# A delta stage whose last two value tiles are convolved among the copies of its join, with three smaller edits

## The reference

```python
# L0 attention: a decaying linear attention; the kernel needs exp(log_decay * distance) for 16 heads
# L1, L2, L3 cross attention, 16 heads, latent keys (64 wide) of 512 positions
scores = jnp.einsum('bhsr,bhlr->bhsl', q_r, k_r)
attn = jax.nn.softmax(scores, axis=-1)
ctx_c = jnp.einsum('bhsl,bld->bhsd', attn, kv_r)
# L2 attention: the gated delta rule
fused_qkv = jax.nn.silu(conv_out)                 # depthwise convolution over 4 tokens
query, key = (l2_norm(query), l2_norm(key))       # 8 heads of 128; value has 16 heads of 128
def step(Sm, inp):
    q_t, k_t, v_t, b_t, a_t = inp
    Sm = Sm * a_t[..., None, None]
    kv = jnp.einsum('bhk,bhkv->bhv', k_t, Sm)
    u = (v_t - kv) * b_t[..., None]
    Sm = Sm + k_t[..., None] * u[:, :, None, :]
    o = jnp.einsum('bhk,bhkv->bhv', q_t, Sm)
    return (Sm, o)
```

## Time and profile before

| | |
|---|---|
| median of 3 runs | 2896.03 us (2892.81 to 2896.42) |
| the profiled execution | 2889.24 us, span 2887.4 us |
| TensorE (PE) busy | 2364.2 us, 82% of the span |
| VectorE (DVE) busy | 1698.7 us, 59% |
| ScalarE (ACT) busy | 1015.2 us, 35% |
| GpSimd (POOL) busy | 769.9 us, 27% |
| mean granted TensorE clock | 0.863 of 2.4 GHz |
| the three latent stages | about 827 to 1083, 1919 to 2184 and 2440 to 2705 us |
| the delta batches | four of about 153.6 us, from about 1229 us |

### The profile page before, as it was taken

How to read it: one execution, slowest core, us unless ns; L and a number is a source line. 1 busy time by engine, 2 the same in 40 slices (tenths; PEclk the granted TensorE clock), 3 DMA queues, 4 the chain that set the end, 5 groups by cost and what they waited for, 6 DMA issues and landing times. The chain is left out here.

```text
span 2887.4 us, 38148 instructions
## 1 busy us (share of the span) xinstructions
PE 2364.2 (82%) x14562; PEld 1587.5 (55%) x14562; DVE 1698.7 (59%) x3527; ACT 1015.2 (35%) x2336; POOL 769.9 (27%) x573
## 2 busy tenths in 40 slices
PE   6797453348999988878889797889998888999899
PEld 4555322114345555657768586745558665555555
DVE  5435986893445652496969687436656753656311
ACT  3132021651035541135444353435552132555210
POOL 1130001000048862110101010028880000888222
PEclk8689555559999999987979797899999958999999
DMA  1000001002000010220101010210001003000411
GB/s 36 19 21 23 0 0 20 1 23 88 0 1 1 1 51 9 107 57 16 44 16 44 16 45 16 51 52 1 1 1 44 21 6 97 1 1 1 121 38 40
DMA packets 100526, 81.77 MB, mean 28 GB/s; under 512 B 52704, under 2 KB 91857, under 8 KB 99770
## 3 DMA queue, kind: packets, MB, share of 16 engines
q1 hardware_dynamic: 99321, 77.89, 9.5%
q0 software_dynamic: 1024, 1.45, 0.2%
HBM read 73.58 MB, written 5.35 MB: 27 GB/s over the span
## 5 line engine op out<-in xcount | busy, mean ns | idle before, releaser
L2032 POOL TENSOR_SCALAR work<-work,small 128x512 f32<-128x512 f32 x384 | 594.3, 1566 | 706.6 <-DVE small L1967 705.3
L2010 ACT ACTIVATE work<-psum,small 128x512 f32<-128x512 f32 x384 | 260.6, 683 | 254.6 <-DVE small L1962 254.6
L1962 DVE TENSOR_REDUCE small<-psum 128x2 f32<-128x1024 f32 x192 | 234.7, 1224 | 176.0 <-PE psum L1912 176.0
L1922 PEld LDWEIGHTS psum<-consts,work 128*128 128x128 f32 x1536 | 165.5, 141 | 114.0 <-issue 101.8
L1912 PE MATMUL psum<-keysT,arena_a 64*128 64x512 f32 x768 | 219.2, 649 | 8.9 <-ACT work L2010 6.0
L1934 PE MATMUL psum<-work,keys 128*64 128x256 f32 x1536 | 187.0, 384 | 36.6 <-issue 34.2
L1922 PE MATMUL psum<-consts,work 128*128 128x128 f32 x1536 | 211.4, 281 | 3.6 <-DVE work L1973 2.6
L1934 PEld LDWEIGHTS psum<-work,keys 128*64 128x64 f32 x1536 | 120.0, 136 | 136.5 <-issue 110.5
L2864 PE MATMUL psum<-xnT,arena_a 128*128 128x256 f32 x512 | 137.4, 423 | 25.8 <-DVE arena_b L3284 23.8
L1973 DVE COPY work<-psum 128x512 f32<-128x512 f32 x192 | 130.9, 682 | 19.7 <-PE psum L1922 19.5
L2017 ACT ACTIVATE work<-psum 128x512 f32<-128x512 f32 x192 | 114.4, 596 | 71.5 <-PE psum L1922 71.5
(11 more groups left out here) (585 smaller groups left out, 4777.6 us busy)
## 6 DMA issues: line engine op xcount, KB each, us to landing
arena_b<-alpha_rows SPq DMA_DIRECT2D x16, 512.0 KB, 5.7
arena_a<-in_L_xattn_Wo SPq DMA_DIRECT2D x3, 2048.0 KB, 13.6
arena_a<-in_L_xattn_Wq SPq DMA_DIRECT2D x3, 2048.0 KB, 13.7
arena_a<-in_L_xattn_w_kc_q SPq DMA_DIRECT2D x3, 1536.0 KB, 12.8
arena_a<-in_L_attn_w_qkv SPq DMA_DIRECT2D x1, 4096.0 KB
arena_a<-in_L_xattn_W_qr SPq DMA_DIRECT2D x3, 768.0 KB
arena_b<-in_L_ffn_w_fc SPq DMA_DIRECT2D x1, 2048.0 KB
arena_b<-in_L_ffn_w_proj SPq DMA_DIRECT2D x1, 2048.0 KB
```

Of the source, the lines that this page charges most:

```text
L1922: mm = nc.tensor.transpose(ps[:, 4 + j, c * P:(c + 1) * P], probs[u % NPB][:, j, c * P:(c + 1) * P], k.c["ident"])
L1962: nc.vector.tensor_reduce(top[:, 2 * u:2 * u + 2], ps[:, u % 2 * 2:u % 2 * 2 + 2, :], AX.X, ALU.max, negate=True).then_inc(*maxed.up())
L2010: nc.scalar.activation(probs[u % NPB][:, j, :], ps[:, u % 2 * 2 + j, :], ACT.Exp, bias=top[:, i:i + 1], accum_out=total[:, i:i + 1]).then_ ...
L2032: nc.gpsimd.tensor_scalar(probs[u % NPB][:, j, :], probs[u % NPB][:, j, :], total[:, i:i + 1], None, ALU.mult).then_inc(*scaled.up())
```

## The change

Four edits.

- Layer 0: the exponential takes half of the exponent instead of an eighth, and two of the three squarings go.
- Latent stages: on even steps ScalarE copies before it exponentiates, on odd steps after it as before.
- Delta, weighting: for key groups 2 and 3 ScalarE multiplies the products by the row's factor out of PSUM (`weigh_keys`, 8 instructions of 128x128 per group), and VectorE multiplies by the decays in one product of 128x1024. Query tile 4 is convolved between groups 2 and 3.
- Delta, late tiles: value tiles 14 and 15 get a place of their own (`late`, over the solve's `X`), so the blocks can be transposed while those two aren't done. Tile 14 is convolved after the transposes and ahead of the first join copy, tile 15 between the first level's copies and the second level's. TensorE turns them ahead of the second level and behind it. To free banks 2 to 5, both halves of a join product now share one bank, all three parts of a closing product another, and the second level uses four banks instead of eight.

```diff
-            k.link(act, nc.scalar.activation(powers, arg, ACT.Exp, scale=0.125), "act")
+            k.link(act, nc.scalar.activation(powers, arg, ACT.Exp, scale=0.5), "act")
...
-            k.link(dve, nc.vector.tensor_tensor(powers, powers, powers, ALU.mult), "dve")
-            k.link(dve, nc.vector.tensor_tensor(powers, powers, powers, ALU.mult), "dve")
             dve.wait_ge(*low.at(1))
...
             for s in range(U + LAG):
+                if s % 2 == 0 and 0 <= s - LAG < U:
+                    keep(s - LAG)
                 if s < U:
                     exps(s)
-                if 0 <= s - LAG < U:
+                if s % 2 == 1 and 0 <= s - LAG < U:
                     keep(s - LAG)
...
+    late = over[:, 3072:4096].rearrange("p (n j s) -> p n j s", n=2, j=2)
...
+        if n < 8:
+            return qkT[:, 2 * pair(n):2 * pair(n) + 2, :]
+        return late[:, n - 14] if n >= 14 else vT[:, (n + 2) % 4]
+
+    def bank_of(n):
+
+        return 3 if n == 15 else n % 3
+
+    def join_bank(g):
+
+        return g if g < 2 else 4 + g
...
                 for r in range(2):
-                    pool.wait_ge(*vturned.at(8 * b + 6 + 2 * r))
+                    pool.wait_ge(*vturned.at(8 * b + 4 + 2 * r))
...
-                    nc.tensor.matmul(ps[0:64, 2 * r, o:o + Q], inv_m[0:32, m, 0:64], J[0:32, m, 0:Q], start=True, stop=True)
-                    mm = nc.tensor.matmul(ps[64:128, 2 * r + 1, o:o + Q], inv_m[64:96, m, 64:128], J[64:96, m, 0:Q],
+                    nc.tensor.matmul(ps[0:64, r, o:o + Q], inv_m[0:32, m, 0:64], J[0:32, m, 0:Q], start=True, stop=True)
+                    mm = nc.tensor.matmul(ps[64:128, r, o:o + Q], inv_m[64:96, m, 64:128], J[64:96, m, 0:Q],
...
                 if r == 0:
-                    pe.wait_ge(*vkept.at(8 * b + 8))
                     pe.wait_ge(*gated.at(8 * b + 8))
...
-                for n in range(10, 16):
+                for n in range(10, 14):
                     turn_values(b, n)
...
                 close_first(b, 0)
                 close_first(b, 1)
+                turn_values(b, 14)
                 for g in range(5):
                     second_level(b, g)
+                turn_values(b, 15)
 
                 for g in range(4):
+                    if g == 0:
+                        pe.wait_ge(*vkept.at(8 * b + 6))
+                    elif g == 2:
+                        pe.wait_ge(*conved.at(16 * b + 15))
+                    elif g == 3:
+                        pe.wait_ge(*vkept.at(8 * b + 8))
...
+            def weigh_keys(b, g):
+                act.wait_ge(*kkd.at(4 * b + g + 1))
+                if g == 2:
+                    act.wait_ge(*negated.at(b + 1))
...
+                            last = nc.scalar.activation(inv[:, h, c * P:(c + 1) * P],
+                                                        ps[:, 4 + g, (2 * j + c) * P:(2 * j + c + 1) * P],
+                                                        ACT.Copy, scale=gn[:, c, h:h + 1])
...
                 silu(b, 3)
+                weigh_keys(b, 2)
                 first_tap(b, 4)
-                act.wait_ge(*normed.at(2 * b + 1))
+                weigh_keys(b, 3)
                 nc.scalar.activation(nk, vs, ACT.Sqrt).then_inc(*rooted.up())
...
             def lower(b, g):
+                if g >= 2:
+                    dve.wait_ge(*weighed.at(2 * b + g - 1))
+                    dve.wait_ge(*scanned.at(8 * b + 2 * g + 2))
+                    nc.vector.tensor_tensor(four(inv, g), four(inv, g), four(decay, g), ALU.mult).then_inc(*lmade.up())
+                    return
...
-                for g in range(4):
+                for g in range(3):
                     lower(b, g)
-                for n in range(4, 8):
+                convolve(b, 4)
+                lower(b, 3)
+                for n in range(5, 8):
                     convolve(b, n)
...
-                for n in range(10, 16):
+                for n in range(10, 14):
                     convolve(b, n)
 
                 turn_blocks(b, 0)
                 turn_blocks(b, 1)
                 for r in range(2):
+                    if r == 0:
+                        convolve(b, 14)
                     dve.wait_ge(*z1d.at(2 * b + r + 1))
...
+                convolve(b, 15)
                 for g in (0, 2):
                     dve.wait_ge(*z2d.at(4 * b + g + 1))
```

More of the change, by code:

```diff
@@ L2792, in delta_batches @@
         sig(n) for n in ("conved", "scanned", "normed", "lmade", "attended", "solved", "xturned", "varred", "froot"))
+    weighed, negated = sig("weighed"), sig("negated")
     squared, cleared, gath, lanes, unlaned, back = (
@@ L2800, in dest @@
     def dest(n):
-        return qkT[:, 2 * pair(n):2 * pair(n) + 2, :] if n < 8 else vT[:, n % 4]
+        if n < 8:
[5 more added lines that the diff above has]
+        return g if g < 2 else 4 + g
     def four(t, g):
```

61 lines of the change are left out of this document (39 added, 22 removed).

## The result

| | |
|---|---|
| before, measured again beside it | 2895.59 us (2892.81 to 2896.42) |
| changed kernel, median of 4 runs | 2824.05 us (2820.33 to 2835.34) |
| ratio | 0.9761, interval 0.973 to 0.9792 |
| its profiled execution | 2835.34 us, span 2833.5 us, mean granted clock 0.863 |

The change gains 71.5 us: 15 more than the forecast of 2839, inside the range.

A forecast was written before the change was run, and what follows sets the result against it. TensorE was taken to set the latent stages' pace, only its idle time winnable. Delta 4 x 5.8 = 23, latent 34, layer 0 nothing: 57 us off 2889.2 gives 2832, plus 6.8 for the median: 2839 us, range 2818 to 2864.

The forecast's parts named there:

- Squarings: Layer 0's attention: removing two VectorE squarings of 2.57 us wins nothing, since the copy behind them waits for a matmul.
- Latent copy order: Latent stages: with ScalarE's copy earlier, all 87 over-keys matmul waits go, -34.2 us; ends 27 and 37.7.
- Weighting and tile 4: Delta batches up to the solve's end: VectorE 1.75 us shorter and its 1.15 us wait gone, -2.9 us.
- Late tiles: Delta batches behind the solve: two value tiles moved later, first join 5.2 us sooner, less costs, -2.9 us in sum.
- T+11.4, T+13.6 and T+18.4: Microseconds after the solve's end in a delta batch: transposes start, first join starts, tile 14's convolution ends.
- TensorE is in the second join until T+20.5: Delta, 20.5 us after the solve's end: the first copy's 1.3 us wait for VectorE therefore costs nothing.
- the same clock of 0.50 in the joins: Sign named for the profile after: delta joins still run at granted clock 0.50.
- The rival of a whole stretch at high clock: Delta joins, closings and level steps run at the higher clock: 19.6 us halved, 9.8 a batch, 2800 us; chance 0.04.
- the other 1.7 us of the bound: Delta upper bound: the first two groups of value products, at half clock before, might win another 1.7 us a batch.
- The latent round shortened: Against the rival that the latent round stays, delayed exponentials (0.36 us) eating the 0.39: delta alone, 2873 us; chance 0.07.
- The delta gain was not given back: Against the rival that levels wait for both late tiles, losing 5.2 of 5.8 us: latent alone, 2862; chance 0.08.
- One bank does not serialise: Against the rival that join and closing products sharing a bank take turns, +15.9 us a batch: 2902 us; chance 0.04.

The follow-up runs named there:

- e2: Kernel before with only layer 0's exponential changed to half the exponent and two squarings removed: 2892.9 us, ratio 0.9991.
- e8: Changed kernel with layer 0's exponential at an eighth of the exponent and the two squarings back: 2824.57 us.
- e1: Kernel before with the latent copy order alone: 2857.83 us, ratio 0.986.
- e6: Kernel before with ScalarE weighting groups 2 and 3 and VectorE's two large products, query tile 4 left behind group 3: 2885.78 us, ratio 0.9972.
- e5: Kernel before with the bank sharing of join and closing products alone, no tile or copy moved: 2896.47 us, ratio 1.0007.
- e9: Changed kernel plus 1, 4, 2, 2 and 2 unread identity products ahead of the five second-level steps' waits, none elsewhere: 2806.22 us, ratio 0.9711.
- e7: Changed kernel plus 25 unread identity products a batch, ahead of the first join, inside joins and closings, and ahead of second-level steps: 2832.8 us, ratio 0.9769.
- e11: As e9, with two more fillers ahead of the first closing: 2804.19 us, ratio 0.9713.

## Why the prediction was right, and where its sizes were off

**Bounds.** That TensorE's idle time, not its work, was to be had, held for the most part: in the profiled pair the span fell by 54 us and TensorE's busy time by 8. The joins, at the higher clock, are the exception: they are work that became shorter.

**Squarings: 0.** Held (e2, e8).

**Latent copy order: 34.2 forecast, 40.1 measured** in the profiled pair (39.6 in e1), above the upper bound of 37.7. The mechanism held: copy first, no wait left, no one else late. The term was mis-sized. I took the 0.39 us of recorded idleness as all that could go. With the copy there early, the over-keys matmuls don't start at the scores' end but 0.08 us before it, in their tail, as the other groups of matmuls in that round do (by 0.06 to 0.17). The forecast had that 0.08 only as a possible cost, in its lower bound. 0.46 times the 87 rounds is 40.

**Weighting and tile 4: 2.9 forecast, 3.1 measured** (51.8 to 48.8). Product 1.21 (forecast 1.2), ScalarE's eight 2.17 to 2.24 (forecast 2.3), the wait gone, the cover of tile 5 0.9 us instead of 0.4. e6 splits it: 2.0 for the smaller work, 1.0 for the place of tile 4.

**Late tiles: 2.9 forecast, 3.9 measured** (44.6 to 40.7; second batch 4.4). T+11.4, T+13.6 and T+18.4 came true to 0.1 us. The next step failed: "TensorE is in the second join until T+20.5". It was done at T+17.8, since the joins had caught the higher clock, and the closings began at T+19.1. That gives 1.4 us in this batch. I had this in the bounds (at 1.1; by the prediction's own T+20.5 and T+19.1 it should have been 1.4), not in the sum, since every window of the old joins is at 0.50. The row ahead of it was the hint: 0.98 from 1473.5 to 1477.5, up to the joins' start. The change brings the joins 5.2 us forward into that stretch. So one sign that the prediction named for itself, the same clock of 0.50 in the joins, failed in all four batches. The rival of a whole stretch at high clock did not come (closings and levels 0.50), and the other 1.7 us of the bound, for the values, didn't either. In the first and the last batch the gain is 3.1 and 3.5 us only: the two closing copies of VectorE (L3472) are 2.9 and 2.7 us apart there, where they were 1.8 and 1.9, as TensorE starts the second closing late, after 0.9 and 0.7 us put down to "issue". What it waits for stays open.

**Sum.** 57 forecast, 66.6 in the stages of the profiled pair, 71.5 in the medians. Six of the gap are the latent term, 3.5 the delta's. The last 5 lie within the spread of the changed kernel's runs, and stay unassigned. Batches are 146.9 us apart on average, for the 147.9 of the forecast. The profiled pair itself is 54 us apart, close to the 57, but that is luck: 66.6 less the 12.7 by which the other stages came out longer.

**Rivals.** The latent round shortened (e1). The delta gain was not given back: of the two late tiles only tile 15 holds a copy up: L3477 starts when that tile is done (1471.38 + 2.68), half a us after TensorE's first level (1.97 us from 1471.58) has ended, which is the 0.5 that was allowed for it. One bank does not serialise (e5). That rival was also priced too low: 192 passes at 0.107 us are 20.5, not 10.3, which makes it 26.1 us a batch and 2943 in all.

## What to carry to other kernels

A wait between two groups of matmuls can be worth more than its recorded idleness (0.46 us for 0.39 here), because once it is gone the groups overlap. Where small dependent matmuls alternate with copies, read the granted clock of that stretch and of the one ahead of it, and ask which of the two the work will stand in once it has moved. Filling the gaps that are idle anyway took 13.6 us off the delta stage, where the late tiles had taken 15.6; fillers inside the chain gave their gain back. Compare stages that a change does not touch before trusting a difference between two totals.

## What was not expected of the hardware

Identical programs differ by their clock. Layer 0's attention is the same in the changed kernel and in e9, and took 128.0 and 120.8 us. Its part from VectorE's small copy on (at 47.8 and at 45.4 us), first in the changed kernel, then in e9:

```profile
47.80:136.65 88.85, 70.71 (x520) 49.04 (x520) 37.87 (x45) 8.25 (x17) 13.22 (x18) 0.68 0.00 1
```

```profile
45.35:129.60 84.25, 64.43 (x520) 44.86 (x520) 37.81 (x44) 8.26 (x17) 13.24 (x18) 0.76 0.00 1
```

The work and the other engines' busy times are alike, TensorE's is 6.3 us apart, and the mean granted clock is 0.68 and 0.76. In this stage it goes up and down between the two levels, at other moments in each execution. That is 4.6 of the 7 us. The other 2.5 lie ahead of the copy, in the first projection (min, median and max in ns):

```profile
L416 PE MATMUL psum<-xnT,arena_a x32: 592/592/1190, 17.6 to 33.2; 128*128 128x512 f32 x32
```

```profile
L416 PE MATMUL psum<-xnT,arena_a x32: 592/592/667, 17.4 to 30.8; 128*128 128x512 f32 x32
```

The changed kernel's first five passes of 32 take 1.06 to 1.19 us, nearly twice the 0.59 of the others; in e9 only the first is longer (0.67). That fits a clock that rose later, though the windows view gives 1.00 for both. For the spread of some 15 us between runs each run's mean granted clock is on record: the changed kernel's four took 2835.3, 2827.7, 2820.4 and 2820.3 us at 0.863, 0.867, 0.869 and 0.870. Time and clock go together, but what the unprofiled runs did in between is not shown.

Full-array fillers inside the joins (TensorE busy 3.95 of 4 us) didn't keep the clock up: in the second batch it fell 4.1 us after the joins' start with them and 4.4 without, which is in the second join with them, as they make it longer, and behind it without them. TensorE was busy all of the next 13.7 us, at 0.50. Between the levels the same products, in e7 and in e9 to e11, go with a clock of 1.00 from 17.5 to 22.3 us after the joins' start on, in every batch; in the changed kernel it is 28.3 to 28.8.
